# Two message-passing layers on one core: TensorE's semaphores raised by a drain behind a group of matmuls

## The reference, cut to what matters

```
s1 = einsum('ea,eb,abc->ec', xs, es, W1) * ...
s2 = einsum('eai,ebi,abc->ec', xv, ev, W2) * ...
v1 = einsum('ea,ebi,abc->eci', xs, ev, W3) * ...
v2 = einsum('eai,eb,abc->eci', xv, es, W4) * ...
agg = segment_sum(tp @ Wm + bm, row)
x = layernorm(x + node + concat([node, agg]) @ Wu + bu)
```

```
h = silu(edge_scalars @ Wfc1);  w = h @ Wfc2
mid0 = w0 * f0[src] * sh0;  mid1 = w3 * (f1[src] . sh1);  mid2, mid3 alike
n0..n3 = segment_mean(mid0..mid3, dst)
x = layernorm(x + sc + alpha * conv)
```

## Time and profile before

| | us |
|---|---|
| median of three runs | 6791.19 |
| lowest, highest | 6786.99, 6808.58 |
| span of the profiled execution, first to last instruction | 6574.9 |
| its busy time: TensorE (PE) | 4404.1 (67%) |
| VectorE (DVE) | 4082.6 (62%) |
| GpSimd (POOL) | 3046.1 (46%) |
| ScalarE (ACT) | 1176.2 (18%) |
| mean granted TensorE clock | 0.753 |

### The profile page before, as it was taken

One profiled execution on the slowest core, in us unless ns is written; L12 is line 12 of the kernel. 1 busy time (PEld: TensorE's weight loads), 2 busy tenths in 40 slices (PEclk: granted clock), 3 DMA queues, 4 the chain that ended last, 5 costly groups with the idle time before them and its releaser, 6 DMA issues. The chain is left out here.

```text
span 6574.9 us, 113593 instructions
## 1 busy us (share of the span) xinstructions
PE 4404.1 (67%) x32521; PEld 3293.8 (50%) x32521; DVE 4082.6 (62%) x7506; ACT 1176.2 (18%) x3413; POOL 3046.1 (46%) x3249
## 2 busy tenths in 40 slices
PE   3767777777776777799776655655655665565555
PEld 2545555555555555689564434444444444444444
DVE  7877778778787766577455445444544544544544
ACT  0322222222222222000120111111111111111111
POOL 0556666566665666100035444444444444444442
PEclk7877778888788777899886666676666667666666
DMA  3333333333333333688332222222222222222221
GB/s 133 94 94 100 94 101 97 98 95 99 94 101 93 101 94 103 216 271 274 119 97 54 48 49 49 48 49 49 49 50 49 48 47 51 48 49 48 50 47 32
DMA packets 602395, 572.30 MB, mean 87 GB/s; under 512 B 183060, under 2 KB 491412, under 8 KB 602308
## 3 DMA queue, kind: packets, MB, share of 16 engines
q0 software_dynamic: 150528, 258.71, 14.5%
q1 hardware_dynamic: 414772, 227.28, 13.7%
q10 hardware_dynamic: 37008, 85.28, 4.2%
HBM read 412.44 MB, written 158.52 MB: 87 GB/s over the span
## 5 line engine op out<-in xcount | busy, mean ns | idle before, releaser
L2299 POOL DMA_INDIRECT q_fg<-f,q_index x1568 | 1484.1, 946 | 1608.8 <-DVE q_prod L2353 1138.1
L1026 POOL DMA_INDIRECT messages<-stage,place x1568 | 1506.8, 961 | 993.3 <-ACT stage L1237 506.4
L2546 PE MATMUL q_ps_m<-q_prod,q_onehot_sh 128*32 128x160 f32 x12544 | 914.4, 426 | 1015.6 <-DVE q_sums L2367 850.2
L1328 PEld LDWEIGHTS ps_m<-by_attr,turned 128*128 128x128 f32 x6272 | 1096.5, 226 | 281.3 <-issue 246.8
L2367 DVE SCALAR_TENSOR_TENSOR q_sums<-q_ps_m,split_q,q_sums 128x161 f32 x784 | 301.2, 384 | 1485.4 <-remote 1294.9
L1328 PE MATMUL ps_m<-by_attr,turned 128*128 128x160 f32 x6272 | 1204.7, 353 | 17.6 <-issue 13.0
L2546 PEld LDWEIGHTS q_ps_m<-q_prod,q_onehot_sh 128*32 128x32 f32 x12544 | 541.7, 150 | 1330.3 <-DVE q_sums L2367 908.4
L1298 PE MATMUL ps_y<-w_xy,xt 32*128 32x256 f32 (+3 forms) x1176 | 476.9, 705 | 488.0 <-ACT xz L1209 250.8
L2533 PE MATMUL q_ps_w<-q_wfc,q_hidden 64*128 64x192 f32 x3136 | 514.6, 425 | 206.6 <-DVE q_prod L2353 145.3
L1237 ACT COPY stage<-ps_m 128x320 f32<-128x320 f32 x784 | 337.2, 435 | 1737.9 <-PE ps_m L1328 848.1
L1118 DVE STREAM_TRANSPOSE by_attr<-by_node 128x2048 f32<-128x2048 f32 (+1 forms) x294 | 548.0, 1915 | 2.7 <-ACT by_node L1212 2.7
(11 more groups left out here) (247 smaller groups left out, 4487.3 us busy)
## 6 DMA issues: line engine op xcount, KB each, us to landing
nat<-in_edge_attr SPq DMA_DIRECT2D x392, 256.0 KB
rows_in<-messages ACTq DMA_DIRECT2D x208, 324.0 KB, 3.4
rows_in<-messages SPq DMA_DIRECT2D x208, 324.0 KB, 3.4
messages<-stage,place POOLq DMA_INDIRECT x1568
q_fg<-f,q_index POOLq DMA_INDIRECT x1568
messages<-zeros ACTq DMA_DIRECT2D x49, 324.0 KB, 2.2
q_a<-in_edge_attr SPq DMA_DIRECT2D x196, 64.0 KB
xw<-in_x SPq DMA_DIRECT2D x98, 80.0 KB
```

Of the source, the lines that this page charges most:

```text
L1026: nc.gpsimd.indirect_dma_start(out=msgs, out_offset=bass.IndirectOffsetOnAxis(ap=place[:, r, k:k + 1], axis=0), in_=stage[:, r, k, :], in_ ...
L1328: last = nc.tensor.matmul(ps_m[g % BANKS][:, k % 2 * D0:k % 2 * D0 + D0], turned[:, r, half, k * P:(k + 1) * P], by_attr[:, r, k, :, half] ...
L2299: nc.gpsimd.indirect_dma_start(out=fg[:, i, place_of(v), :], out_offset=None, in_=f_tab, in_offset=bass.IndirectOffsetOnAxis(ap=index[:, i ...
L2546: nc.tensor.matmul(ps_m[strip, 0:D0], oh_sh[:, strip], prod[:, h % 2, g * QUAD + place_of(v), 1 if c < 3 else 0, :], start=(v == 0), stop= ...
```

## The change: what it does

In seven functions of TensorE, `then_inc` is taken off the last matmul of the group, and `pe.drain().then_inc(...)` stands behind the group. A drain is an instruction in TensorE's queue that waits for the matmuls ahead of it, then raises the semaphore; TensorE's instructions behind it stand behind it in the queue. Nothing is changed in the matmuls, in their order, in the waits, or in any other engine.

```diff
@@ turn (s_xt_ps), step_a, step_b, step_c (s_y)
-    nc.tensor.matmul(ps_y[2][0:NV, P:2 * P], xw[:, r, P:D0], sel[:, r, :], ...).then_inc(s_xt_ps, 1)
+    nc.tensor.matmul(ps_y[2][0:NV, P:2 * P], xw[:, r, P:D0], sel[:, r, :], ...)
+    pe.drain().then_inc(s_xt_ps, 1)
...
-    product(ps_y[2], 0, XY, W12, xt, w_xy).then_inc(s_y, 1)
+    product(ps_y[2], 0, XY, W12, xt, w_xy)
+    pe.drain().then_inc(s_y, 1)
@@ messages
-    last.then_inc(s_msg, 1)
+    pe.drain().then_inc(s_msg, 1)
@@ hidden_layer, edge_weights, node_sums
-    last.then_inc(s_h, 1)
+    pe.drain().then_inc(s_h, 1)
...
-    last.then_inc(s_wt, 1)
+    pe.drain().then_inc(s_wt, 1)
...
-    last.then_inc(s_m, 1)
+    pe.drain().then_inc(s_m, 1)
```

More of the change, by code:

```diff
@@ L1294, in turn @@
                             nc.tensor.matmul(ps_y[2][:, 0:P], xw[:, r, 0:P], sel[:, r, :], start=True, stop=True)
-                            nc.tensor.matmul(ps_y[2][0:NV, P:2 * P], xw[:, r, P:D0], sel[:, r, :], start=True, stop=True).then_inc(s_xt_ps, 1)
+                            nc.tensor.matmul(ps_y[2][0:NV, P:2 * P], xw[:, r, P:D0], sel[:, r, :], start=True, stop=True)
+                            pe.drain().then_inc(s_xt_ps, 1)
                         def product(bank, at, rows, cols, source, weights):
@@ L1313, in step_b @@
                             product(ps_y[1], 0, XX, W34, xt, w_xy)
-                            product(ps_y[2], 0, XY, W34, xt, w_xy).then_inc(s_y, 1)
+                            product(ps_y[2], 0, XY, W34, xt, w_xy)
+                            pe.drain().then_inc(s_y, 1)
                         def step_c(n):
@@ L1318, in step_c @@
                             product(ps_y[0], 0, XS, W34, xt, w_xy)
-                            product(ps_y[0], 256, XZ, W34, xz, w_z).then_inc(s_y, 1)
+                            product(ps_y[0], 256, XZ, W34, xz, w_z)
+                            pe.drain().then_inc(s_y, 1)
                         def messages(n, r, g):
@@ L1327, in messages @@
                                 for half in range(2):
-                                    last = nc.tensor.matmul(ps_m[g % BANKS][:, k % 2 * D0:k % 2 * D0 + D0], turned[:, r, half, k * P:(k + 1) * P],
-                                                            by_attr[:, r, k, :, half], start=(half == 0), stop=(half == 1))
-                            last.then_inc(s_msg, 1)
+                                    nc.tensor.matmul(ps_m[g % BANKS][:, k % 2 * D0:k % 2 * D0 + D0], turned[:, r, half, k * P:(k + 1) * P],
+                                                     by_attr[:, r, k, :, half], start=(half == 0), stop=(half == 1))
+                            pe.drain().then_inc(s_msg, 1)
                         def epoch(t, r, ahead=True):
@@ L2522, in hidden_layer @@
                             rows = slice(a // 2 * 64, a // 2 * 64 + 64)
-                            last = nc.tensor.matmul(ps_h[:, a // 2, a % 2 * P:a % 2 * P + P], wfc1[rows, a % 2, :], scal_t[rows, par, :],
+                            nc.tensor.matmul(ps_h[:, a // 2, a % 2 * P:a % 2 * P + P], wfc1[rows, a % 2, :], scal_t[rows, par, :],
                                                     start=True, stop=True, tile_position=(a // 2 * 64, 0))
-                        last.then_inc(s_h, 1)
+                        pe.drain().then_inc(s_h, 1)
                     def edge_weights(k, par, g):
@@ L2532, in edge_weights @@
                                 rows = slice(64 * half, 64 * half + 64)
-                                last = nc.tensor.matmul(ps_w[:, g, half, b, 0:192], hidden[rows, par, 2 * g + b, :], wfc2[rows, :],
+                                nc.tensor.matmul(ps_w[:, g, half, b, 0:192], hidden[rows, par, 2 * g + b, :], wfc2[rows, :],
                                                         start=True, stop=True, tile_position=(64 * half, 0))
-                        last.then_inc(s_wt, 1)
+                        pe.drain().then_inc(s_wt, 1)
                     def node_sums(k, h, g, ones):
@@ L2548, in node_sums @@
                         pe.wait_ge(s_hsum, k + 1)
-                        last = nc.tensor.matmul(ps_m[96:P, D0:W1_], hot_sum[:, h, g, :], counted[:, ones:ones + 1],
+                        nc.tensor.matmul(ps_m[96:P, D0:W1_], hot_sum[:, h, g, :], counted[:, ones:ones + 1],
                                                 start=False, stop=True, tile_position=(0, 96))
-                        last.then_inc(s_m, 1)
+                        pe.drain().then_inc(s_m, 1)
                     def features(i, half, k):
```

## The result

The changed kernel takes 7305.62 us (median of four executions, 7289.66 to 7329.08), the kernel before on the same chip 6789.09 (6786.42 to 6808.58). The ratio is 1.0764 [1.0732, 1.0795]: 517 us slower. The forecast was 5833 us and faster; the value lies above the range too. The one rival that lands close is "held up just the same, and TensorE with it", at 7388.

A forecast was written before the change was run, and what follows sets the result against it. Matmul-raised semaphores held up during GpSimd's indirect DMAs were taken as the bound. Gains of 737 us (second layer) and 221 us (message stage) off the 6574.9 us span, plus 216.3 us carried over, gave 5833 us; range 5400 to 7150.

The forecast's parts named there:

- held up just the same, and TensorE with it: Rival, both stages: completion itself is late, so drains sit until GpSimd's series ends and stop TensorE; 7388 us, chance 15%.
- What is late: Both stages: semaphores raised by matmuls are held up, by up to some 8 us, while GpSimd makes indirect DMA descriptors.
- prompt: Both stages: a drain's update isn't held up as a matmul's is; the likeliest case, 5833 us, chance 57%.
- The rival's sum: Both stages, completion late and TensorE stopped: 310 + 123 us of moved work and 164 us of bared drains, 597 us added.
- 1.58 x 196 = 310: Second layer: hidden layer and edge weights, 1.58 us a batch, would come behind the hold instead of inside it.
- 123 and 66: Message stage: 123 us for one of two groups moved behind the hold each epoch, 66 us for bared drains.
- the first rival: TensorE becomes the bound: drains work but each bares 0.74 us, and more pauses can slow its clock; 6627 us, chance 9%.
- The drain's price: TensorE, each drain: 0.40 us of bared tail and restart where group follows group, 0.14 where a pause exists already.
- The 216.3 us "around the span": Whole kernel: the runs' median lay 216.3 us above the profiled span of 6574.9; carried over onto the forecast span of 5617.
- Forecast of 23.0 and 12.0 us: Message stage from 25.25 to 23.0 us an epoch, gaining 221; second layer from 15.76 to 12.0 a batch, gaining 737.
- Only the drains' cost: Rival, both stages: updates stay late or lateness isn't the cause, TensorE goes on; 164 us added, 6955 us, chance 14%.
- no change: Rival: drains fall where TensorE waits anyway and the updates stay late; 6791 us, chance 5%.

The follow-up runs named there:

- e4: Kernel before, with the second layer's indirect gathers replaced by plain DMAs of as many rows: 5352.52 us, ratio 0.8158.
- e3: Kernel before, matmuls keeping their semaphore updates, with a bare drain added behind each group in both stages: 7297.03 us, ratio 1.0740.
- e5: Changed kernel (drains in both stages), with the second layer's indirect gathers replaced by plain DMAs: 5697.3 us, ratio 0.8683 to the kernel before.
- e12: The changed kernel itself, run again later where it met no holds: 5113.36 us, ratio 1.0109 to the kernel before.
- e11: Kernel before, with a GpSimd memset as a pause behind each second-layer gather, run without holds: 5466.76 us, ratio 1.0812.
- e8: Kernel before, with the message stage's indirect writes replaced by plain DMAs, run without holds: 5012.38 us, ratio 0.9913.
- A: Set of follow-up runs on one chip, testing the drains by stage and bare drains; kernel before had a median of 6798.1 us.
- B: Set of follow-up runs on one chip, testing plain gathers and waits for landing; kernel before had a median of 6561.65 us.
- E: Set of follow-up runs on one chip, the kernel before and pauses behind gathers; kernel before had a median of 6789.65 us.
- C: Set of follow-up runs on one chip, testing plain message writes, waits for landing and pauses; kernel before had a median of 5058.04 us.
- D: Set of follow-up runs on one chip, the changed kernel, pauses and plain message writes; kernel before had a median of 5056.95 us.
- e17: Kernel before, with a GpSimd memset as a pause behind each second-layer gather, run beside holds: 6365.32 us, ratio 0.9380.
- e9: Changed kernel (drains in both stages), with plain DMAs for the message stage's indirect writes, run without holds: 5096.81 us, ratio 1.0079 to the kernel before.
- e14: Kernel before, with plain DMAs for the message stage's indirect writes, repeated in a later set without holds: ratio 0.9902.
- e15: Changed kernel, with plain DMAs for the message stage's indirect writes, repeated in a later set without holds: ratio 1.0079 to the kernel before.

## Why the prediction was wrong, by its own steps

**What is late: right.** That TensorE's signals, and not VectorE or the sums, hold the second layer up, and that this comes from the indirect DMAs, is borne out by e4: take the indirect gathers away and the add's wait falls from 1295 to 156 us.

**The step that failed: "Completion is there; the message of it is late. I take 'prompt'."** The earlier trace rows show that weight loads begin 0.74 us behind a step inside a series. I read that as TensorE knowing that its matmuls are done. It shows only that the next instruction may enter; no row before shows what a drain waits for. After, the drain of 7.1 us and the 6.01 us idle behind it show that it waits for just the completion that is late, and e3 shows it with the updates left where they were. By its own proof ("gaps of 5 us and more before TensorE's next weight load while GpSimd issues") the rival "held up just the same, and TensorE with it" is the one that happened. I gave it 15%, with the evidence for "prompt" a single row on another event.

**The rival's sum, 597 us, against 519: right in all, less so in its parts.** For the second layer it had 1.58 x 196 = 310 for the work moved behind the hold and 98 for bared drains, 408; measured 245. For the message stage 123 and 66, 189; measured 274. The first is too high, though the hidden layer does stand behind a hold in nearly every batch (169 of 196). The rival counts all of the 1.58 us as lost, but in the timeline after the hidden layer (4015.99) and the add (4016.05) start together, so a part is hidden; and it prices bared drains at 0.40 us, which was too much. How the 163 us divide between the two isn't shown. The second is too low. It moves one group of two and leaves out the clock: the drains of the message stage were held for 322 us together, and 46% of the message matmuls ran at the lower clock level for 27% before (mean granted clock 0.75 for 0.79, mean matmul of L1332 394 ns against 353). TensorE's work grew from 18.7 to 22.0 us an epoch. What the holds and the clock are worth apart isn't shown; the clock is what the first rival had named. In the second layer it is 0.61 for 0.66.

**The drain's price: far too high.** I took 0.40 and 0.14 us. Unheld it is 0.12 us in the second layer of e5, and 26 ns over the whole kernel in e12. So of the 517 us some 56 are drains and 461 holds, with the lower clock that comes with them; the split assumes that a drain costs the same in both kinds of run, which none could test.

**The 216.3 us "around the span": wrong.** They were no fixed part of an execution but the distance between a profiled execution of another kind and the median. Span and time differ by 1.7 us after.

**Forecast of 23.0 and 12.0 us.** Without holds the changed kernel has 21.6 us an epoch and 10.1 a batch (e12: 1800 us for 1334, 1900 us for 1501). So the periods came out near, and on the slow side, but the change earns nothing there: the code before has 21.4 us an epoch (e11: 1800 us for 1343) and 10.0 a batch (e8) without holds. TensorE's terms were too high: 9.30 us of work a batch was read at a clock of 0.67, where e12 has 7.6 at 0.81. What the sums priced was a kernel without holds, which this change does not make.

**"Only the drains' cost" (6955) and "no change"** fall by the idle time behind the drains. The Trainium skill's 26.3 ns for each increment by a matmul ("TensorE: Matmul & The Clock Gate", section "The cost: per-tile semaphore tail") is no measure of it beside a hold; where nothing is held (e4) the semaphore behind the sums rises some 0.05 us after the last matmul's modelled end, and nothing there contradicts it.

## What stays open

Why the same kernel meets holds in some sets (A, B, E) and none in others (C, D), with the program alike, and the chip's number alike in A and D. Set B, with holds, is still 3.5% quicker than A. Whether the held matmuls' data are late or only their acknowledgement can't be told, since a matmul's end is modelled. What the held completion is queued behind: the more indirect transfers a series had, the later the release after its end. By the semaphore events of the trace before it came, in the second layer, 1.1 to 1.3 us behind a series of 4, 1.7 to 1.8 behind 8 and 1.9 to 2.3 behind 11, as if each transfer added some 0.14 us to a backlog at a pitch of 1.25 us; in the message stage it was 1.4 behind 8 and 2.5 behind 15, but 2.3 behind the series of 4, which doesn't fit. With the pitch at 1.49 (e17) it came some 0.5 us behind a series of 4, and mostly inside one of 12, which fits; but holds were left. That is an inference, not a proof. That the message stage's holds come from its own indirect writes is argued from the second layer: plain writes with holds beside them were never measured, since the runs of e8, e9, e14 and e15 met none. And e4 changes two things at once, the kind of the DMA and how long each keeps GpSimd (787.93/1488 = 0.53 us for 0.95).

## What to carry to other kernels

A drain does not make a completion come sooner; it makes its engine wait for it. If a semaphore comes late, first find out whether the completion or its message is late, by one kernel that keeps the update and adds a bare drain, and take the cause away (here the indirect DMAs) rather than the place where the update hangs. And before summing on one profiled execution, set its span beside the median: if they differ by per cents, its rows may not be those of the runs to be predicted. And before calling a long drain a hold, look at the clock it ran at.

## What the runs showed of the hardware

- Beside a series of indirect DMAs on GpSimd the completion of TensorE's matmuls can be late, not only its report to other engines: drains behind the sums ended up to 8.9 us after the last matmul (0.10 us at most in e12), and one of L2539 ended 14.9 us after it, beside GpSimd's opening series.
- It isn't always so: the same kernel took 5057 us and 6798 us on chips of the same number, 34% apart, each repeated within 0.9% in its set. Removing one stage's indirect gathers was worth 18.4% where there were holds.
- A drain behind a group costs 26 to 39 ns net over the whole kernel when nothing is held (e12, e9), though its record is 1.04 us long or more: most of it overlaps the matmuls ahead. Behind the same eight matmuls it is 1.39 us at the full clock and 2.50 at the lower level.
